# Two-layer LoRA residual kernel: the adapter ids are loaded by SP ahead of the first block of x, no longer by GpSimd

## The chip, the cores and the metric

One core of one Trainium2 chip runs the kernel. The metric is the device time of one execution in microseconds (us), taken as the median of several runs.

## The reference, cut to what matters

The input `x` has 8 batch rows of 512 tokens with 2048 features. Two residual steps follow each other. In the first, every batch row picks one of 8 small adapters (rank 16), by its entry in `itok_B_3_7`. In the second, there is a shared dense 2048 x 2048 product and a rank-16 adapter picked by `itok_B_0_15`.

```python
# step 0
Bx  = einsum('bni,bri->bnr', x, B0[ids0])
x   = x + einsum('bnr,bor->bno', Bx, A0[ids0])
# step 1
xr  = einsum('bsi,bir->bsr', x, lora_A[ids1])
x   = x + einsum('bsi,io->bso', x, W) + einsum('bsr,bro->bso', xr, lora_B[ids1])
```

So the program has to know the 16 integers `ids0` and `ids1` before it can fetch any adapter matrix. They are 8 int32 values each, 32 bytes.

## The kernel before, in words

**Tiling.** The 8 batch rows are worked in 4 pairs (`PAIRS`). For each pair, the dense product is a seven-product scheme in the manner of Strassen (`P1, P2, P6, P7, P4, P3, P5`, in this order), and each product has 8 units (`UNITS`). The identity is added to W's diagonal blocks, so that x + xW is one product. A unit is 24 matmuls of 128x128 by 128x512 in the loop of L1024. Every operand is split into a high and a low part in float32r: ScalarE casts the high part (`w_hi` L555, `b_hi` L566), VectorE subtracts to get the low part (`w_lo` L708, `b_lo` L721), and three matmuls stand for one.

**Folding step 0 in.** In the first pair, products P1, P2, P7 and P4 carry extra matmuls: `p_mm` (L997) multiplies the block of W that is in SBUF by the adapters A0 of all 8 batch rows side by side (`a0_hi`, `a0_lo`), and `in_mm` (L955) multiplies the chosen B0 and A1 by x into `lr_ps`. `p_mm` of unit 0 stands directly behind the 24 matmuls of unit 0 in TensorE's program. It waits for `a0_ready`, which VectorE gives after `a0_split` (L784), which follows ScalarE's `a0_split` (L582), which waits for all eight A0 loads together (`a0_loaded` at 16 * NB).

**Who loads what.** There is one order per engine, written out by hand.

- GpSimd (POOL) builds `eye` (L312, L314), loads the ids (L385, L386), waits for both, then reads each id into a register (`value_load`, L318 and L321) and issues one load for it: 8 loads of A0 (L389, 128 KB each, written into `a0_raw`, which is a view of `u3`; the profile calls it `u`), two loads of `in_raw` (L327), 8 loads of A1 (L393). Later come eight late A0 loads (L417), eight copies of B1 from HBM to HBM (L420), and the stores of the results.
- SP issues all loads of x (`load_x`, L442) and of W (`load_raw`, L480), each 512 KB. The program begins with x block 0, W block 0, x 1, W block 2, x 2, W block 1, x 3, W block 3. The W blocks go through a ring of four buffers `w_raw` (`RAWS`). In the first eight units each unit takes two of them: its own block, and a second one that VectorE turns into a difference (`w_second`, L714), that SP stores to HBM (`store_sum`, L487) for later use. The buffer of the second block is loaded again when that store has landed, and SP waits for it in order.

**VectorE around the change.** Before unit 0: the diagonal sum (L703), the low parts of x 0 and W 0 (L721, L708), then `w_second(0)` (L714), which needs W block 1. Then for unit 1: the diagonal sum, `w_lo`, `b_lo`, four small operations that build the base of `j_raw` (L894 to L901), and then `a0_split` twice and `in_split` (L799).

The two lines that move stand in GpSimd's program; the wait behind them stays:

```python
            pool.dma_start(ids[:, 0, :], ids0).then_inc(ids_loaded, 16)
            pool.dma_start(ids[:, 1, :], ids1).then_inc(ids_loaded, 16)
            pool.wait_ge(ids_loaded, 32)
```

Of the kernel before, what the change touches and what calls it, by code (L numbers as in the profile page):

```python
# [35 lines left out]
def lora_residual_program(nc, xT, ids0, ids1, A0n, B0, W, A1, B1, yT):  # L36
    NB = ids0.shape[1]
    NA0, _, C, R = A0n.shape
    NA1 = B1.shape[0]
    N = xT.shape[3]  # L40
# [112 lines left out]
    with ExitStack() as ctx:  # L153
        def sb(name, shape, dt=F32):
            return ctx.enter_context(nc.sbuf_tensor(name, shape, dt))
# [4 lines left out]
        def sem(name):  # L160
            return ctx.enter_context(nc.semaphore(name))
# [36 lines left out]
        ids = sb("ids", [1, 2, NB], I32)  # L198
# [11 lines left out]
        ids_loaded = sem("ids_loaded")  # L210
# [100 lines left out]
        def _(pool):  # L311
# [18 lines left out]
            def load_lr(i):  # L330
                p, b, half, _ = lr_plan[i]
                if i == 0:
                    pool.wait_ge(b1_copied, 16 * NB)
                    pool.wait_ge(a0_ready, 4 * len(P_PRODUCTS))
                else:
                    pool.wait_ge(lr_ready, i)
                for h in ((0, 1) if b else (half,)):
                    for g in range(2):
                        pool.wait_ge(*stage_free(stage_at["pst", h, g]))
                for c in range(4):  # L340
                    pool.dma_start(lr_raw[2 * R * c:2 * R * (c + 1), :], lrw[2 * p + b, :, half * HD:(half + 1) * HD]  # L341
                                   ).then_inc(lr_loaded, 16)
                if (b, half) == (1, 0):
                    for s in range(2):
                        last = max(k for k, (kind, q, _) in enumerate(stage_plan) if k % STAGES == s and q <= p
                                   or k % STAGES == s and kind == "pst")
                        pool.wait_ge(*stage_free(last))
                    for c in range(4):
                        pool.dma_start(lr_more[2 * R * c:2 * R * (c + 1), :], lrw[2 * p + b, :, HD:D]
                                       ).then_inc(lr_more_loaded, 16)  # L350
# [31 lines left out]
                pool.wait_ge(*bank_free(tile(p, P5, m)))  # L382
                pool.dma_start(yT[(2 * p + 1) * C + m, :, :], u2[:, m, :]).then_inc(u2_stored[m], 16)

            pool.dma_start(ids[:, 0, :], ids0).then_inc(ids_loaded, 16)  # L385
            pool.dma_start(ids[:, 1, :], ids1).then_inc(ids_loaded, 16)  # L386
            pool.wait_ge(ids_loaded, 32)
            for b in range(NB):
                pool.dma_start(a0_raw[:, b, :, :], A0n[bass.ds(id0(b), 1), :, :, :].rearrange("a p c r -> (a p) c r")  # L389
# [46 lines left out]
        def _(sp):  # L436
            def load_x(p, i, j):
                if p:
                    user = {X11: P5, X12: P7, X21: P4, X22: P3}[i]
                    sp.wait_ge(x_ready, 4 * ((p - 1) * PRODUCTS + user) + j + 1)  # L440
                half, b = divmod(i, 2)
                sp.dma_start(x_raw[i][:, 2 * j:2 * j + 2, :], xT[(2 * p + b) * HC + 4 * half + j, :, :, :]  # L442
                             ).then_inc(x_loaded[i][j], 16)
# [17 lines left out]
            def load_raw(r):  # L461
                n = raw_plan[r]
                p, o, u = at(n)
                if r >= RAWS:
                    raw_free(r - RAWS)
                block = {P1: A11, P2: A12, P6: A22, P4: A22, P3: A12, P5: A21}.get(o)
                kind = {P6: None if p == 0 else S2, P7: S3}.get(o)
                if raw_of[n] != r:
                    block = {P1: A21, P5: A22}.get(o)
                    kind = {P6: S3, P3: S2}.get(o)  # L470
                if kind is None:
                    src = W[block, u, :, :, :]
                else:
                    if kind == S3:
                        k = raw_of[u] + 1
                        sp.wait_ge(w_stored[k % RAWS], 16 * s3_stores[k])
                    else:
                        sp.wait_ge(s2_stored[u % 2], 16 * (u // 2 + 1))
                    src = w_sum[kind, u, :, :, :]
                sp.dma_start(w_raw[r % RAWS][:, :, :], src).then_inc(w_loaded[r % RAWS], 16)  # L480
# [8 lines left out]
            def load_fix(q):  # L489
# [4 lines left out]
                sp.wait_ge(*stage_free(stage_at["c21" if q >= UNITS else "c11", 0, q % UNITS]))  # L494
                sp.dma_start(stage[s % STAGES][:, :], c_kept[q, :, :]).then_inc(fix_loaded[s % STAGES], 16)

            load_x(0, X11, 0)
            load_raw(0)
            load_x(0, X11, 1)
# [183 lines left out]
        def _(dve):  # L683
# [167 lines left out]
            def fix(q):  # L851
                s = stage_at["fix", 1, q]
                dve.wait_ge(fix_loaded[s % STAGES], 16 * sum(k == "fix" for k, _, _ in stage_plan[s % STAGES:s + 1:STAGES]))
                dve.wait_ge(fix_mm_done, q + 1)
                dve.tensor_tensor(stage[s % STAGES][:, :], (j_ps, p_ps)[q % 2][:, :], stage[s % STAGES][:, :], ALU.add
                                  ).then_inc(fix_done, 1)
# [232 lines left out]
```

## Time and profile before

| | |
|---|---|
| median of 3 runs | 1403.8 us (1402.41 to 1404.17) |
| profiled execution, its own time | 1402.34 us |
| span of the profiled execution | 1400.7 us |
| TensorE busy | 1367.2 us, 98% of the span |
| VectorE, ScalarE, GpSimd busy | 58%, 29%, 12% |
| mean granted TensorE clock | 0.993 |
| mean DMA traffic | 187 GB/s |

TensorE is busy in all of the span but some 33 us by the first line (matmul records overlap and some can be missing, so the waits are read from the waits' own view). The span runs from the first to the last instruction; the profiled execution took 1.6 us more than its span. Engines are PE (TensorE matmul), PEld (its weight load), DVE (VectorE), ACT (ScalarE), POOL (GpSimd) and SP. A "q" behind a name is the engine's instruction queue, where DMA issues, register loads and waits are handled. "Landing" is the time from a DMA's issue to its semaphore.

### The profile page before, as it was taken

To read this page: it belongs to the slowest core of one execution; us is meant where nothing else is said; L and a number is where in the kernel's file an instruction comes from. 1 tells how busy PE (TensorE), PEld (TensorE's weight loads), DVE (VectorE), ACT (ScalarE), POOL (GpSimd) and SP (SyncE) were. 2 spreads that over 40 slices of the span, in tenths; PEclk is the share of its full clock that TensorE was granted. 3 is DMA by queue.
4 is the path that set the end of the run, shared out by engine and by line. 5 is a ranking of instruction groups with operands and counts; after the bars stand their busy time and mean duration, and the time that the engine had idled before them with its cause. 6 is when DMAs were issued, how large, how long until landed. Compare 5 with 4: busy or idle time off the path is not lost.

```text
span 1400.7 us, 15653 instructions
## 1 busy us (share of the span) xinstructions
PE 1367.2 (98%) x6016; PEld 1129.2 (81%) x6016; DVE 810.2 (58%) x941; ACT 405.9 (29%) x462; POOL 165.0 (12%) x317
## 2 busy tenths in 40 slices
PE   5999999999999999999999999999999999999997
PEld 4888888888878888888887888888887888888886
DVE  3455855357776455646775555555766445554675
ACT  2332222223234223322332323232322422232230
POOL 3200100111123010012011010012012001001202
PEclk8999999999999999999999999999999999999999
DMA  8864843458887343357684252446785334234755
GB/s 303 310 225 134 299 158 113 153 186 280 294 280 240 122 136 120 129 195 246 236 289 146 86 173 96 151 151 213 256 297 187 99 120 135 91 91 133 223 201 180
DMA packets 76778, 261.81 MB, mean 187 GB/s; under 512 B 12176, under 2 KB 12176, under 8 KB 76576
## 3 DMA queue, kind: packets, MB, share of 16 engines
q1 hardware_dynamic: 57600, 205.55, 43.5%
q0 software_dynamic: 19104, 55.27, 11.7%
q8 instruction: 48, 0.79, 0.2%
q14 instruction: 26, 0.21, 0.0%
HBM read 213.52 MB, written 48.30 MB: 187 GB/s over the span
## 4 chain that ended last, share of the span: by engine, by line
PE 85%; DVE 5%; DMA 5%; ACT 2%; issue 2%; POOL 0%; POOLq 0%; SPq 0%; ACTq 0%; DVEq 0%
PE y_ps L1024 76%; PE lr_ps L955 4%; PE p_ps L997 3%; DMA w_raw<-in_W 2%; PE y_ps L976 2%; ACT w_hi L555 2%; DVE w_lo L708 1%; DVE w_raw L694 1%; DVE b_lo L721 1%; DMA w_raw<-w_sum 1%; DVE u L776 1%; DMA stage_all<-lrw 0%; DMA u<-in_A0n 0%; DVE u L777 0%; DVE val L835 0%
## 5 line engine op out<-in xcount | busy, mean ns | idle before, releaser
L1024 PE MATMUL y_ps<-b_hi,w_hi 128*128 128x512 f32 x1792 | 699.3, 390 | 15.3 <-DVE w_lo L708 8.8
L1024 PE MATMUL y_ps<-b_lo,w_hi 128*128 128x512 f32 x1792 | 698.6, 390 | 0.0
L1024 PE MATMUL y_ps<-b_hi,w_lo 128*128 128x512 f32 x1792 | 698.4, 390 | 0.0
L708 DVE TENSOR_TENSOR w_lo<-w_raw,w_hi 128x1024 fp32r<-128x1024 f32 x216 | 264.6, 1225 | 460.9 <-ACT w_hi L555 460.9
L555 ACT CAST w_hi<-w_raw 128x1024 fp32r<-128x1024 f32 x216 | 227.6, 1054 | 879.5 <-PE y_ps L1024 474.9
L1024 PEld LDWEIGHTS y_ps<-b_hi,w_hi 128*128 128x128 f32 x1792 | 337.3, 188 | 86.6 <-DVE w_lo L708 8.8
L1024 PEld LDWEIGHTS y_ps<-b_hi,w_lo 128*128 128x128 f32 x1792 | 337.2, 188 | 70.2
L1024 PEld LDWEIGHTS y_ps<-b_lo,w_hi 128*128 128x128 f32 x1792 | 337.3, 188 | 70.1
L721 DVE TENSOR_TENSOR b_lo<-x_raw,b_hi 128x1024 fp32r<-128x1024 f32 x112 | 136.5, 1219 | 0.0
L566 ACT CAST b_hi<-x_raw 128x1024 fp32r<-128x1024 f32 x112 | 117.5, 1049 | 2.4 <-DMA x_raw<-in_xT 2.4
L694 DVE TENSOR_TENSOR w_raw<-w_raw 128x1024 f32<-128x1024 f32 x64 | 78.1, 1221 | 19.5 <-DMA w_raw<-in_W 11.6
L377 POOL DMA_DIRECT2D out_y<-stage_all x64 | 34.9, 546 | 413.9 <-DVE stage_all L760 377.9
L760 DVE TENSOR_TENSOR stage_all<-y_ps,u 128x512 f32<-128x512 f32 x64 | 43.1, 688 | 20.8 <-PE y_ps L976 16.9
L955 PE MATMUL lr_ps<-b_hi,in_stk 128*128 128x512 f32 x128 | 50.4, 394 | 0.0
L955 PE MATMUL lr_ps<-b_lo,in_stk 128*128 128x512 f32 x128 | 50.3, 393 | 0.0
L381 POOL DMA_DIRECT2D out_y<-u x32 | 17.6, 548 | 260.1 <-DVE u L776 259.5
L769 DVE TENSOR_TENSOR u<-y_ps,u 128x512 f32<-128x512 f32 x64 | 41.1, 685 | 7.4 <-PE y_ps L1024 5.0
L976 PE MATMUL y_ps<-val,lr_w 128*128 128x512 f32 x112 | 44.0, 393 | 1.3 <-DVE val L835 1.1
L327 POOL DMA_DIRECT2D in_raw<-in_B x8 | 4.5, 563 | 307.6 <-issue 307.6
L341 POOL DMA_DIRECT2D lr_raw<-lrw x64 | 31.4, 497 | 76.1 <-DVE lr_w L817 68.6
L997 PE MATMUL p_ps<-w_hi,a_hi 128*128 128x512 f32 x64 | 26.0, 407 | 8.2 <-DVE a_lo L784 8.2
L955 PEld LDWEIGHTS lr_ps<-b_hi,in_stk 128*128 128x128 f32 x128 | 24.5, 191 | 5.2
(81 smaller groups left out, 605.8 us busy)
## 6 DMA issues: line engine op xcount, KB each, us to landing
w_raw<-in_W SPq DMA_DIRECT2D x208, 512.0 KB, 3.8
w_raw<-w_sum SPq DMA_DIRECT2D x96, 512.0 KB, 3.6
x_raw<-in_xT SPq DMA_DIRECT2D x64, 512.0 KB, 5.4
out_y<-u POOLq DMA_DIRECT2D x64, 256.0 KB, 6.4
out_y<-stage_all POOLq DMA_DIRECT2D x64, 256.0 KB, 3.4
lr_raw<-lrw POOLq DMA_DIRECT2D x64, 128.0 KB, 4.0
w_sum<-w_raw SPq DMA_DIRECT2D x8, 512.0 KB, 6.2
c_kept<-stage_all POOLq DMA_DIRECT2D x16, 256.0 KB, 3.2
```

The source lines that it names most:

```text
L377: pool.dma_start(dst, stage[s % STAGES][:, :]).then_inc(stage_stored[s % STAGES], 16)
L555: act.copy(w_hi[n % 2][:, :, :], w_tile(n)[:, :, :]).then_inc(w_hi_done, 1)
L566: act.copy(b_hi[:, 2 * j:2 * j + 2, :], x_raw[i][:, 2 * j:2 * j + 2, :]).then_inc(x_hi_done, 1)
L694: last = dve.tensor_tensor(raw[:, :, :], w_raw[main_raw(n)][:, :, :], w_raw[r % RAWS][:, :, :], ALU.subtract if o == P3 else ALU.add)
L708: dve.tensor_tensor(w_lo[n % 2][:, :, :], w_tile(n)[:, :, :], w_hi[n % 2][:, :, :].bitcast(F32), ALU.subtract).then_inc(w_ready, 1)
L721: dve.tensor_tensor(b_lo[:, 2 * j:2 * j + 2, :], x_raw[i][:, 2 * j:2 * j + 2, :], b_hi[:, 2 * j:2 * j + 2, :].bitcast(F32), ALU.subtract). ...
L760: dve.tensor_tensor(stage[s % STAGES][:, :], bank[:, :], (u2 if o == P2 else u3)[:, m, :], ALU.add).then_inc(added, 1)
L769: dve.tensor_tensor(u2[:, m, :], bank[:, :], u2[:, m, :], ALU.add).then_inc(added, 1)
L955: last = pe.matmul(lr_ps[:, :], cols, x[:, c, :], start=(first and c == 0 and x is b_hi), stop=(half == 1 and c == HC - 1 and x is b_lo))
L976: return pe.matmul(out[:, :], lr_w[i % 2][:, m * P:(m + 1) * P], val[b][:, :], start=start, stop=True)
L997: last = pe.matmul(p_ps[:, :], a0[:, 2 * j + c, :], w[n % 2][:, c, :], start=(j == 0 and c == 0 and k == 0), stop=(j == 3 and c == 1 and k ...
L1024: last = pe.matmul(bank[:, :], w[n % 2][:, c, t * P:(t + 1) * P], x[:, 2 * j + c, :], start=(j == 0 and c == 0 and w is w_hi and x is b_hi ...
```

## The change

The two loads of the ids leave GpSimd's program. SP issues them, ahead of everything else. GpSimd's wait for `ids_loaded` stays where it was, and nothing else is different. Line numbers behind the removed lines are lower by two in GpSimd's part and in the part of SP ahead of the inserted lines.

```diff
@@ GpSimd
-            pool.dma_start(ids[:, 0, :], ids0).then_inc(ids_loaded, 16)
-            pool.dma_start(ids[:, 1, :], ids1).then_inc(ids_loaded, 16)
             pool.wait_ge(ids_loaded, 32)
             for b in range(NB):
...
@@ SP
+            sp.dma_start(ids[:, 0, :], ids0).then_inc(ids_loaded, 16)
+            sp.dma_start(ids[:, 1, :], ids1).then_inc(ids_loaded, 16)
             load_x(0, X11, 0)
             load_raw(0)
             load_x(0, X11, 1)
```

GpSimd's order at its start, before. `TENSOR_LOAD ids` is the read of one id into a register, and `u` is the A0 buffer:

```order
L314 AFFINE_SELECT eye<-eye 128x128
L385 DMA ids<-in_ids 1x8x1
L386 DMA ids<-in_ids 1x8x1
L318 TENSOR_LOAD ids
L318 ISA x2
L389 ISA
L389 DMA u<-in_A0n 128x256
```

and with the change:

```order
L314 AFFINE_SELECT eye<-eye 128x128
L318 TENSOR_LOAD ids
L318 ISA x2
L387 ISA
L387 DMA u<-in_A0n 128x256
L318 TENSOR_LOAD ids
```

The two DMA issues between `eye` and the first read of an id are gone from GpSimd.

SP's order at its start, before:

```order
L435 UNCONDITIONAL_BRANCH
L442 DMA x_raw<-in_xT 128x1024
L480 DMA w_raw<-in_W 128x1024
L442 DMA x_raw<-in_xT 128x1024
L480 DMA w_raw<-in_W 128x1024
L442 DMA x_raw<-in_xT 128x1024
```

and with the change:

```order
L433 UNCONDITIONAL_BRANCH
L495 DMA ids<-in_ids 1x8
L496 DMA ids<-in_ids 1x8
L440 DMA x_raw<-in_xT 128x1024
L478 DMA w_raw<-in_W 128x1024
L440 DMA x_raw<-in_xT 128x1024
```

Every x and W load of SP stands behind two more issues. The orders of TensorE, VectorE and ScalarE are the same in both kernels.

## Rows read from the trace of the kernel before

**Rows 1.** The page: busy time, share of the span, instructions of TensorE
```profile
PE 1367.2 (98%) x6016; PEld 1129.2 (81%) x6016; DVE 810.2 (58%) x941; ACT 405.9 (29%) x462; POOL 165.0 (12%) x317
```

**Rows 2.** The three largest waits of TensorE: total us, times, longest us
```profile
PE y_ps L1024 <- DVE w_lo L708: 8.8, 1, 8.8
PE p_ps L997 <- DVE a_lo L784: 8.2, 1, 8.2
PE y_ps L1024 <- DVE u L777: 6.4, 3, 2.2
```

**Rows 3.** Chain of waits, first 84 us: start us, us, what
```profile
2.31 5.29 DMA ids<-in_ids
...
17.54 6.19 DMA u<-in_A0n
...
24.19 0.44 DVE a_lo L784
...
24.67 2.92 PE p_ps L997 x6
...
35.18 1.36 PE p_ps L997 x6
```

**Rows 4.** Timeline of GpSimd: start us, us, what, [idle before <-releaser]
```profile
2.31 0.55 POOL L386 DMA_DIRECT2D ids<-in_ids  x1
9.10 0.59 POOL L389 DMA_DIRECT2D u<-in_A0n  x1 [6.25 <-issue]
...
30.29 0.54 POOL L393 DMA_DIRECT2D u<-in_A  x1 [1.57 <-issue]
```

**Rows 5.** Timeline of SP's queue
```profile
0.94 0.38 SPq L442 DMA_DIRECT2D x_raw<-in_xT  x1
...
1.85 0.42 SPq L442 DMA_DIRECT2D x_raw<-in_xT  x1
...
12.72 3.90 SPq L480 DMA_DIRECT2D w_raw<-in_W  x2
...
27.09 0.33 SPq L487 DMA_DIRECT2D w_sum<-w_raw  x1
```

**Rows 6.** Timeline of ScalarE
```profile
4.61 1.04 ACT L566 CAST b_hi<-x_raw 128x1024 fp32r<-128x1024 f32 x1 [2.40 <-DMA x_raw<-in_xT]
...
38.78 1.05 ACT L589 CAST lr_w<-u 128x1024 fp32r<-128x1024 f32 x1
...
60.39 1.05 ACT L555 CAST w_hi<-w_raw 128x1024 fp32r<-128x1024 f32 x1 [6.87 <-PE p_ps L997]
```

**Rows 7.** Landing times of the eight A0 loads (L389)
```profile
DMA to landing us min/median/max: 3.3/4.6/6.2
```

**Rows 8.** Timeline of VectorE
```profile
11.09 1.23 DVE L714 TENSOR_TENSOR w_raw<-w_raw 128x1024 f32<-128x1024 f32 x1 [2.30 <-DMA w_raw<-in_W]
...
14.98 1.22 DVE L721 TENSOR_TENSOR b_lo<-x_raw,b_hi 128x1024 fp32r<-128x1024 f32 x1
...
16.70 0.24 DVE L901 COPY j_raw<-j_raw 128x64 f32<-128x64 f32 x1
...
57.57 0.49 DVE L703 TENSOR_TENSOR w_raw<-w_raw,eye 128x128 f32<-128x128 f32 x2 [1.65 <-DMA w_raw<-in_W]
```

**Rows 9.** Timeline of TensorE: the last matmul of unit 0
```profile
16.09 0.39 PE L1024 MATMUL y_ps<-b_hi,w_lo 128*128 128x512 f32 x1
```

**Rows 10.** Stretches: us; PE, PEld, DVE, ACT, POOL busy; granted clock, DMA share, GB/s
```profile
9.00:12.00 3.00, 3.00 (x8) 2.35 (x9) 0.91 (x1) 0.00 (x0) 1.68 (x3) 1.00 1.02 416
...
24.70:29.70 5.00, 5.00 (x12) 3.93 (x13) 3.13 (x5) 2.50 (x5) 2.15 (x4) 0.50 0.65 182
30.00:34.00 4.00, 4.00 (x19) 3.29 (x18) 2.54 (x3) 0.00 (x0) 1.87 (x4) 1.00 1.01 363
...
402.10:405.30 3.20, 3.20 (x8) 2.52 (x9) 1.69 (x3) 0.28 (x1) 2.31 (x5) 0.50 0.93 278
430.00:1380.00 950.00, 944.74 (x4163) 780.64 (x4162) 556.14 (x633) 283.36 (x313) 97.26 (x186) 1.00 0.51 170
```

## The prediction, made before the changed kernel ran

> **What bounds the kernel now.** I read the page first. TensorE is busy for 98% of the span [rows 1], so time is only to be had where TensorE waits, or where its clock is halved. The second view was the list of its waits [rows 2]: 8.8 us before the first matmul, 8.2 us at the first `p_mm`, 6.4 us in three pieces at the ends of pairs. What follows in the list is smaller than any of these. After 24.67 us TensorE runs through the rest of the program with little more than 6.4 us of waits, so an early gain should reach the end unless a buffer or a load is late in its turn.
>
> The third view was the chain of waits in the first 84 us [rows 3]. The wait of 8.2 us ends last on this chain: GpSimd issues the second ids load at 2.31; it takes 5.29 us to land, until 7.60; GpSimd reads an id and issues a load of A0 for it, eight times, the first at 9.10 [rows 4] and the eighth at 17.54; the eighth takes 6.19 us to land; ScalarE and VectorE split it; `p_mm` starts at 24.67. TensorE's last matmul of unit 0 was issued at 16.09 and done at 16.48 [rows 9]. So the ids stand at the head of the only long wait in the program's middle, and this is where the change acts.
>
> **The change, step by step.** *Removed from GpSimd:* two issues, the second of 0.55 us [rows 4]. They lie wholly inside its wait for the ids and cost nothing by themselves; what counts is when the second lands.
>
> *Added to SP:* two issues ahead of x. SP starts at 0.94, and the x loads at 0.94 and 1.85 have one W issue between them, so two issues take 0.91 us [rows 5]. The second ids load is thus issued near 1.40, and everything of SP moves by 0.91 us. The first matmul waits for x 0 and W 0 with nothing to cover it: 8.8 [rows 2] becomes 9.7, and unit 0 ends at 17.4 in place of 16.48 [rows 9]. This cost is hidden as long as `p_mm` starts later than 17.4; if A0 were there by then, 0.91 us would be the price.
>
> *When the ids land.* The trace has no small load on SP's queue. Nearest is the first x load, also at the head of that queue: issued at 0.94, its reader ScalarE starts at 4.61 [rows 5, 6], so 3.67 us, of which its 524 kB take 1.3 us at 416 GB/s [rows 10]. That leaves 2.4 us for one of 32 bytes. From the other side: the 5.29 us that the same bytes take now. I take 2.4, because the x row shares queue, place and an idle start, while the ids of before go beside 512 KB loads. So the ids land near 3.8 (bounds 3.8 and 6.7), 3.8 us before 7.60.
>
> *The A0 loads.* GpSimd's own pace does not change, so the eighth is issued at 17.54 - 3.8 = 13.7. Its landing takes 3.3 to 6.2 us, median 4.6 [rows 7]; `p_mm` starts 0.94 us behind it (17.54 + 6.19 = 23.73, and 24.67 [rows 3]). That gives 17.9 to 20.8, with the median 19.2.
>
> *VectorE's own order, which is late next.* Its `a0_split` stands behind its work for unit 1. That begins with `w_second(0)` at 11.09, which waited for W block 1, and ends with the last `j_raw` copy at 16.94 [rows 8], 5.85 us later. W block 1 is the sixth load of SP. It moves by 0.91 us, and by the A0 bytes that now go in front of it: some 6 loads of 131 kB at 416 GB/s, 1.9 us (bounds: none, and all eight, 2.5 us). Hence 11.09 + 0.91 + 1.9 = 13.9, VectorE free for A0 at 19.75, and `p_mm` 0.48 us later (a_lo at 24.19 to 24.67 [rows 3]): 20.2, between 18.3 and 20.8. Both chains end near each other, and the later one counts. **I take 20.4.** TensorE resumes 24.67 - 20.4 = **4.3 us earlier**, and its gap shrinks from 8.2 to 3.0 us. The cover of what was moved past is then thin, but there: b_lo of unit 1 was done at 16.2 [rows 8] and comes at 19.0, while unit 1's matmuls start after `p_mm` and `in_mm`, past 22.
>
> *The clock.* After the 8.2 us gap TensorE works at half clock (1.2 of 2.4 GHz): granted 0.50 from 24.70 to 29.70 and 1.00 from 30.00 on [rows 10], and six `p_mm` matmuls take 2.92 us where they take 1.36 later [rows 3]. The half-clock stretch reaches from 24.67 to some point between 29.7 and 30, 5.2 us, of which half, 2.6 us, is lost. What a 3.0 us gap does is not shown. Below it there are the three gaps of 2.0 to 2.2 us at pair ends [rows 2]: the first was followed by 3.2 us or a little more at 0.50, the other two lie in a stretch with a granted clock of 1.00 throughout [rows 10]. So the loss is between 0 and 2.6 us. I take the stretch of the nearest gap that had one, 3.4 us, 1.7 us lost. That is a gain of **0.9 us** (bounds 0 and 2.6). If the clock stays up, `in_mm` waits some 0.3 us for `in_split`, which stands behind `a0_split`.
>
> *The rest.* GpSimd's A1, late A0 and B1 loads come 3.8 us earlier by the clock, TensorE's need of them 5.2 us earlier. A1 is needed first: its last load was issued at 30.29 [rows 4] and ScalarE read it at 38.78 [rows 6]. Now the issue is at 26.5, and the read comes 5.2 us earlier, at 33.6: 7.1 us between them, more than any of the A0 landings. So this costs nothing. The W ring is a rival below.
>
> *Sum.* 4.3 + 0.9 = 5.2 us. The profiled execution would take 1402.34 - 5.2 = 1397.1. It was 1.5 us quicker than the median of the runs, so the median becomes 1403.8 - 5.2 = **1398.6 us**. A measurement of this kernel can tell about 0.2%, 2.8 us, from no change; 1401.0 and 1406.6 are the borders.
>
> **Rivals.**
>
> *The clock stays up* (chance 0.23). The 3.0 us gap is no fall, as with two of the three gaps at pair ends. Gain 4.3 + 2.6 - 0.3 = 6.6 us: 1397.2. Against it speaks that a gap of 2.0 us was enough once [rows 2, 10].
>
> *The ids are hardly earlier* (chance 0.15): a load of one row takes its 5.3 us on whatever queue, because the time lies in the round trip and not in the traffic beside it. Then they land at 1.40 + 5.3 = 6.7, 0.9 us earlier; `p_mm` starts near 23.7, and the gap of 6.3 us still halves the clock: 1402.9, no change. For it: no row shows how much of the 5.29 us was traffic. Against it: the x load's 3.67 us in total. The Trainium skill ("DMA: Bandwidth & Descriptors", Specifications) puts the two queues' first bytes only some 0.4 us apart, about 1 us and 0.6 us. By that page alone, an estimate, the ids would come 0.9 + 0.4 = 1.3 us earlier and the kernel would take about 1402.5. No row has a small load on both queues, so the trace neither agrees nor disagrees.
>
> *The W ring decides* (chance 0.06), the one on the other side. In the first eight units each buffer of a second block waits for a store to land before it is loaded again. VectorE already waited 1.65 us for W block 12 at 57.57; its sum was done at 58.06, and the cast that needs it was released by TensorE at 60.39 [rows 6, 8]: 2.3 us of cover. In this rival the ring is paced by DMA, not by TensorE. It starts 0.9 us later, has 1.9 us of A0 traffic in front of its first reload (at 12.72 before [rows 5]), and the B1 copies now overlap it more. As soon as block 12 is over 2.3 us later than before by the clock, all that was gained at 20 us is waited for there; 1.2 us more and a new half-clock stretch of 3.4 us (1.7 us lost) give 1403.8 + 1.2 + 1.7 = 1406.7. Against it: SP issued its last reload by 16.6 and the x load behind it, and then nothing until 27.09 [rows 5], waiting for VectorE, which waited for A0. That part of the ring moves forward with the change.
>
> **How the numbers follow.** Forecast (short gap, one short half-clock stretch): 0.56. Clock up: 0.23. Ids hardly earlier: 0.15, of which 0.05 for landings in between that still give over 2.8 us. Ring: 0.06, of which 0.02 for a loss that only eats the gain. Faster: 0.56 + 0.23 + 0.05 = 0.84; within: 0.10 + 0.02 = 0.12; slower: 0.04. The range: at best both chains end early (19.2, a gain of 5.5) and the clock stays up (2.6 - 0.3): 7.8 us, 1396.0. At worst within 8 in 10, the ids land halfway between the bounds (5.2, so 1.5 us later than I take) and the clock gives nothing: 4.3 - 1.5 = 2.8 us, 1401.0; I add 0.5 us, since the three runs lie 1.8 us apart. Range 1395.9 to 1401.5.
>
> **What would show it.** In the profile of the changed kernel: ids issued at about 0.94 and 1.40, landing after 2.4 us each; the first A0 load at 5.3 and the eighth at 13.7; the first matmul at 9.7; `w_second(0)` at 13.9; `p_mm` at 20.4, released by VectorE, behind a gap of 3.0 us; a half-clock stretch of about 3.4 us or none; no other wait of TensorE before the first pair's end. It would be wrong if the ids landed after 5.2, if `w_second(0)` began after 16, or if waits of TensorE for w_lo appeared between 28 and 75 us.

## The result, and the profile after

| | before | changed |
|---|---|---|
| median of 20 runs each | 1402.68 us | 1398.18 us |
| lowest and highest | 1399.11 to 1407.09 | 1392.75 to 1404.54 |
| profiled execution, own time | 1402.34 us | 1396.92 us |
| its span | 1400.7 us | 1395.3 us |

The ratio of changed to before is 0.9969, with a 95% interval of 0.9956 to 0.9981: a gain of 4.3 us, between 2.7 and 6.2. The changed kernel is faster, by less than the spread of single runs.

The waits of TensorE in the changed kernel (total us, times, longest), to be read against [rows 2]:

```profile
PE y_ps L1024 <- DVE w_lo L708: 9.6, 1, 9.6
PE y_ps L1024 <- DVE u L777: 6.8, 3, 2.5
PE p_ps L997 <- DVE a_lo L784: 2.3, 1, 2.3
PE y_ps L976 <- DVE val L835: 0.8, 2, 0.6
```

The wait at `p_mm` went from 8.2 to 2.3 us, the one before the first matmul grew from 8.8 to 9.6. The others are nearly as they were.

The timeline of SP's queue and of GpSimd (start us, us, what), against [rows 4, 5]:

```profile
0.94 0.34 SPq L495 DMA_DIRECT2D ids<-in_ids  x1
1.33 0.22 SPq L496 DMA_DIRECT2D ids<-in_ids  x1
1.60 0.36 SPq L440 DMA_DIRECT2D x_raw<-in_xT  x1
...
4.05 0.71 POOL L387 DMA_DIRECT2D u<-in_A0n  x1 [2.56 <-issue]
...
12.09 0.54 POOL L387 DMA_DIRECT2D u<-in_A0n  x1 [0.61 <-issue]
```

The ids' landing has no row of its own here, but GpSimd's reads of the ids show when they were there. The group of these reads on the tile `ids`, with its minimum, median and maximum in ns and its first and last start:

```profile
L318 POOLq TENSOR_LOAD <-ids x9: 288/294/501, 2.5 to 12.1; - x9
```

The first read is at 2.5 us, 1.2 us after the second ids load was issued. Before, it was at 7.6. All A0 loads follow over 5 us earlier: the first at 4.05 in place of 9.10, the eighth at 12.09 in place of 17.54.

The timeline of VectorE, against [rows 8]:

```profile
13.24 1.23 DVE L714 TENSOR_TENSOR w_raw<-w_raw 128x1024 f32<-128x1024 f32 x1 [3.73 <-DMA w_raw<-in_W]
...
18.85 0.20 DVE L901 COPY j_raw<-j_raw 128x64 f32<-128x64 f32 x1
18.96 0.75 DVE L784 TENSOR_TENSOR a_lo<-u,a_hi 128x256 fp32r<-128x256 f32 x2
...
56.62 0.49 DVE L703 TENSOR_TENSOR w_raw<-w_raw,eye 128x128 f32<-128x128 f32 x2 [3.02 <-DMA w_raw<-in_W]
...
66.42 0.49 DVE L703 TENSOR_TENSOR w_raw<-w_raw,eye 128x128 f32<-128x128 f32 x2 [3.62 <-DMA w_raw<-in_W]
```

VectorE goes from the `j_raw` copy straight into `a0_split`, with no idle time between them. So its own order sets `p_mm` now, not the landing of A0. That order begins with the landing of W block 1, which the chain of waits shows:

```profile
3.91 9.31 DMA w_raw<-in_W
13.22 0.02 issue
13.24 1.23 DVE w_raw L714
```

The last two rows of the timeline are the W ring at units 6 and 7: VectorE waits 3.0 and 3.6 us there for W blocks, where unit 6 had 1.65 us in [rows 8].

The stretches of TensorE's granted clock around `p_mm`, in the columns of [rows 10]:

```profile
19.50:20.20 0.70, 0.70 (x3) 0.60 (x4) 0.21 (x1) 0.24 (x1) 0.24 (x1) 1.00 1.02 392
20.40:23.60 3.20, 3.20 (x8) 2.11 (x8) 2.74 (x4) 2.20 (x4) 1.38 (x4) 0.50 0.95 346
23.80:30.00 6.20, 6.20 (x29) 5.11 (x28) 2.79 (x4) 0.18 (x1) 2.32 (x6) 1.00 0.86 308
```

After a gap of 2.3 us the first three matmuls run at the full clock, then the clock is halved for some 3.4 us.

**Where the gain is, along the program.** The chain of waits gives the start of each piece of TensorE's work. In the changed kernel:

```profile
19.43 2.21 PE p_ps L997 x6
21.64 1.96 PE lr_ps L955 x4
23.60 5.59 PE y_ps L1024 x24
...
31.46 5.44 PE y_ps L1024 x24
...
69.42 5.69 PE y_ps L1024 x24
...
79.00 5.44 PE y_ps L1024 x24
```

and before:

```profile
29.30 5.87 PE y_ps L1024 x24
...
37.44 5.44 PE y_ps L1024 x24
...
75.39 5.46 PE y_ps L1024 x24
...
84.75 5.44 PE y_ps L1024 x24
```

The lead of the changed kernel, by how much earlier it starts the same piece, is 5.24 us at `p_mm` (24.67 against 19.43), 5.70 at unit 1, 5.98 at unit 2 once the clock is back in both, 5.97 at unit 7, 5.75 at the first unit of P2, and 5.4 at the end. Unit 7 takes 5.69 us where it took 5.46: the first 0.2 us are lost there, in a short wait for `w_lo` that the list of waits above does not have:

```profile
69.36 0.19 PEld L1024 LDWEIGHTS y_ps<-b_hi,w_hi 128*128 128x128 f32 x1 [0.38 <-DVE w_lo L708]
```

### The profile page after: what moved, and what is told of

Same layout as the page of the kernel before. It is cut to its first block, busy times and chain, and to the rows that moved or that the text cites. A ratio compares the mean times of both kernels' runs of the same rounds, so it can differ in the third digit from the quotient of the medians.

```text
span 1395.3 us, 15653 instructions
## 1 busy us (share of the span) xinstructions
PE 1366.9 (98%) x6016; PEld 1128.3 (81%) x6016; DVE 810.1 (58%) x941; ACT 404.9 (29%) x462; POOL 163.3 (12%) x315
## 4 chain that ended last, share of the span: by engine, by line
PE 84%; DVE 7%; DMA 4%; ACT 2%; issue 2%; SPq 0%; POOLq 0%; POOL 0%; ACTq 0%; DVEq 0%
PE y_ps L1024 74%; PE lr_ps L955 4%; PE p_ps L997 3%; DMA w_raw<-in_W 3%; ACT w_hi L555 2%; DVE w_lo L708 2%; DVE w_raw L694 2%; PE y_ps L976 2%; DVE b_lo L721 1%; DVE u L776 1%; DVE u L777 1%; DMA w_raw<-w_sum 1%; DVE w_raw L703 0%; DVE val L835 0%; PE j_ps L1005 0%
## 5 line engine op out<-in xcount | busy, mean ns | idle before, releaser
L694 DVE TENSOR_TENSOR w_raw<-w_raw 128x1024 f32<-128x1024 f32 x64 | 78.2, 1221 | 19.7 <-DMA w_raw<-in_W 12.2
L703 DVE TENSOR_TENSOR w_raw<-w_raw,eye 128x128 f32<-128x128 f32 x96 | 23.5, 287 | 14.0 <-DMA w_raw<-in_W 13.3
```

What stands on the lines that cost most here:

```text
L694: last = dve.tensor_tensor(raw[:, :, :], w_raw[main_raw(n)][:, :, :], w_raw[r % RAWS][:, :, :], ALU.subtract if o == P3 else ALU.add)
```

## The experiments

**Is it the queue or the traffic?** *The ids on GpSimd, as its first work.*

```diff
+            pool.dma_start(ids[:, 0, :], ids0).then_inc(ids_loaded, 16)
+            pool.dma_start(ids[:, 1, :], ids1).then_inc(ids_loaded, 16)
             pool.memset(eye[:, :], 1.0).then_inc(eye_done, 1)
...
-            pool.dma_start(ids[:, 0, :], ids0).then_inc(ids_loaded, 16)
-            pool.dma_start(ids[:, 1, :], ids1).then_inc(ids_loaded, 16)
```

> GpSimd issues the ids loads as its first work, ahead of building eye (which it did before them), so about 0.7 us earlier than in the kernel before and ahead of the first bytes of x; x stays where it was. Theory traffic (the ids were slow because x and W were moving beside them): the first issue comes near 0.93, the second near 1.6; the second still lands with traffic beside it from about 3.3 us on, so GpSimd reads the first id between 4.5 and 6 us, not at 7.6. Rival queue (a small load of GpSimd takes 5 us whatever moves): read at 1.6 + 5.3 = 6.9 us. In either case the first matmul stays at 8.8 us.

Measured: GpSimd issued them at 1.5 and 2.15 us, hardly earlier than before (1.62 and 2.31). The chain shows 5.13 us of landing for the second, the first read came at 7.31, and `p_mm` at 23.78. One run took 1403.85 us. The numbers look like the rival's, but the traffic beside the load was the same as before, so this run does not tell the two apart. It does show that the place in GpSimd's order is worth 0.3 us.

*SP issues nothing before the ids of GpSimd have landed.*

```diff
+            sp.wait_ge(ids_loaded, 32)
             load_x(0, X11, 0)
             load_raw(0)
```

> The kernel before, with one wait added: SP issues nothing until the ids of GpSimd have landed. This measures a GpSimd load of 32 bytes with nothing beside it, and costs the first matmul what it takes. Theory traffic: the second ids load (issued at 2.31) lands after 2 to 2.5 us, near 4.5 us; SP's first issue is then at 4.5, the first matmul at 12.5, the first A0 load at 6. Rival queue: it lands at 7.6 as before, SP's first issue is at 7.6, the first matmul at 15.5.

The chain of waits of this kernel:

```profile
2.31 1.60 DMA ids<-in_ids
```

against 2.31 and 5.29 in [rows 3]. The same engine, queue, bytes and time of issue, and 1.6 us in place of 5.3 with nothing beside it. **Some 3.7 us of the ids' landing was traffic.** SP's first issue came at 3.93, the first matmul at 11.79, the first A0 load at 5.42, `p_mm` at 22.0. The rival falls. The one execution took 1399.92 us, with the first matmul 3.0 us later than before and `p_mm` 2.7 us earlier.

*The ids on SP, behind x block 0 and W block 0.*

```diff
-            sp.dma_start(ids[:, 0, :], ids0).then_inc(ids_loaded, 16)
-            sp.dma_start(ids[:, 1, :], ids1).then_inc(ids_loaded, 16)
             load_x(0, X11, 0)
             load_raw(0)
+            sp.dma_start(ids[:, 0, :], ids0).then_inc(ids_loaded, 16)
+            sp.dma_start(ids[:, 1, :], ids1).then_inc(ids_loaded, 16)
```

> The changed kernel, with the two ids loads of SP behind x block 0 and W block 0 in place of ahead of them. Theory traffic: the ids are issued near 1.9 and 2.2 with 1 MB in front of them and land behind it, near 6 us; first matmul at 8.85; first A0 load at 7.6, eighth at 15.7, p_mm near 21.5. Rival queue (SP's queue is quick for small loads wherever they stand): they land 1.2 us after issue, near 3.5; first A0 load at 5, p_mm at 18.8, and this order would beat the change by 0.7 us.

```profile
2.22 3.90 DMA ids<-in_ids
```

The same queue as in the changed kernel, 0.9 us later in it, and 3.90 us in place of 1.2. The first A0 load was at 7.68, the eighth at 15.72, `p_mm` at 22.10, the first matmul at 8.80, and the one execution took 1399.38 us. So the place ahead of x is what makes SP's load quick.

**What does SP's delay cost?** *The kernel before, with SP loading the ids a second time into a buffer that nobody reads.*

```diff
+            sp.dma_start(ids_x[:, 0, :], ids0).then_inc(ids_x_loaded, 16)
+            sp.dma_start(ids_x[:, 1, :], ids1).then_inc(ids_x_loaded, 16)
             load_x(0, X11, 0)
...
```

> The kernel before, where SP loads the ids into a spare buffer that nobody reads, ahead of x. This is the cost of the change without its benefit. Theory (the delay of SP is hidden behind the wait for A0): first matmul at 9.5 us (8.8 plus two issues), ids read by GpSimd at 7.6 or up to 0.7 later, p_mm at 24.7, time as before. Rival (the two issues are paid in full): p_mm and the end come 0.7 us later.

The first matmul came at 9.47. But `p_mm` did not stay at 24.7: it came at 22.32. The chain shows where the 2.35 us are:

```profile
2.31 4.36 DMA ids<-in_ids
...
17.22 4.16 DMA u<-in_A0n
```

GpSimd's own ids loads landed 0.9 us sooner, of which 0.3 are left at the issue of the eighth A0 load (17.22 against 17.54). The other 2.0 us are the landing of that load, 4.16 us in place of 6.19. That x, issued 0.66 us later, left them less traffic is a likely reason, but one execution does not show it. The delay of SP is hidden, as the theory had it. The one run took 1404.63 us, inside the range of the kernel before.

This also bounds what the ids are worth. The three profiles with the ids on GpSimd's queue beside SP's x have `p_mm` at 24.67, 23.78 and 22.32. The two with SP's ids first and the same work behind them (the changed kernel, and below the one with x12 and x22 later) have it at 19.43 and 19.54. The profile before is the latest of the first three, because its eighth A0 load took the longest to land. So of the 5.24 us at `p_mm` up to 2.35 may belong to that execution and not to the place of the ids.

**Is VectorE late because of the A0 bytes?** *GpSimd holds A0 back until `w_second(0)` is done.*

```diff
             pool.wait_ge(ids_loaded, 32)
+            pool.wait_ge(postsum_done, 1)
```

> The changed kernel, where GpSimd issues no A0 load before VectorE has finished w_second(0), so that no A0 byte moves ahead of W block 1. Theory (in the changed kernel the A0 bytes in front delay W block 1 by some 1.5 us): w_second(0) starts at 11.09 + 0.66 = 11.75 us, not at 13.24. TensorE then waits for A0 instead: first A0 load near 14.5, p_mm near 29, and the time is some 9 us worse than the changed kernel. Rival (it is later for another reason, such as slower DMA in this run): w_second(0) stays near 13.2.

```profile
12.00 1.23 DVE L715 TENSOR_TENSOR w_raw<-w_raw 128x1024 f32<-128x1024 f32 x1 [2.46 <-DMA w_raw<-in_W]
```

`w_second(0)` starts at 12.00 in place of 13.24 (the line number is one higher here): A0 in front of W block 1 costs 1.2 us. That is 0.25 us later than expected. `p_mm` came at 26.57, earlier than the 29 expected, since the eighth A0 load landed within 2.3 us of its issue at 23.37 in place of over 5. The execution took 1406.11 us.

**Does VectorE's order set `p_mm`?** *The `j_raw` operations one unit later.*

```diff
-                    if n == 0:
+                    if n == 1:
                         half = j_raw[:, :, :, :]
```

> The changed kernel, with the four small VectorE operations on j_raw (0.8 us) moved from unit 0's turn to unit 1's, so that a0_split does not stand behind them. Theory (in the changed kernel VectorE's own order sets p_mm, not A0): p_mm starts at 18.6 in place of 19.4 us, released by a_lo; about 0.8 us gained there, which no timing resolves (within 0.2% of the changed kernel). Rival (the A0 landing at 17.4 is the limit): p_mm stays at 19.4.

The waits of TensorE that differ, and the clock from 17 to 30 us:

```profile
PE p_ps L997 <- DVE a_lo L784: 1.1, 1, 1.1
PE lr_ps L955 <- DVE in_stk L799: 1.1, 1, 1.1
```

```profile
17.00:30.00 13.00, 10.86 (x47) 8.34 (x46) 8.31 (x15) 4.17 (x8) 5.36 (x10) 1.00 0.94 349
```

`p_mm` starts at 18.77, 0.66 us earlier, so VectorE's order was the limit. TensorE then waits at `in_mm`, because `in_raw` is the next load to be late. In these 13 us the clock did not fall (later it did, at the first pair's end: 0.50 from 397.1 to 400.3), and the span was 1392.4 us. Timed, it took 1397.67 us (10 runs), 0.9965 of before (0.9952 to 0.9978): not to be told from the changed kernel.

**Another idle engine.** *The ids on ScalarE's queue.*

```diff
-            sp.dma_start(ids[:, 0, :], ids0).then_inc(ids_loaded, 16)
-            sp.dma_start(ids[:, 1, :], ids1).then_inc(ids_loaded, 16)
...
+            act.dma_start(ids[:, 0, :], ids0).then_inc(ids_loaded, 16)
+            act.dma_start(ids[:, 1, :], ids1).then_inc(ids_loaded, 16)
             w_split_first = -1
```

> The ids are loaded by ScalarE, which is idle at the start; SP's and GpSimd's programs have no ids load. Theory (what counts is that nothing moves beside them yet, not that SP does it): GpSimd reads the first id near 2.5 us as in the changed kernel, and SP's x is not delayed: first matmul at 8.85 and not 9.56, w_second(0) at 12.6 and not 13.2, p_mm at 18.8 and not 19.4. The time is 0.6 us better than the changed kernel, 4 to 5 us better than before. Rival (x's issue beside it makes the ids slow again): read of the id after 4 us, p_mm after 20.

The rival held for the read: issued at 0.9 and 1.5 us, with SP's x issued at the same time, the ids were read at 4.4 us and not at 2.5. The first matmul was at 8.77, `w_second(0)` at 11.35, and `p_mm` at 19.89, now behind the A0 landing. The ratio was 0.9986 (0.9970 to 1.0002), median 1401.22 in 12 runs: a gain is not shown, and the runs reached from 1394.2 to 1404.7.

> The kernel with the ids on ScalarE's queue once more, for a second profile, since its runs ranged from 1394 to 1405. If the ids' landing is a matter of chance there (their issue lies beside x's first bytes), the read of the first id moves by over 0.5 us against 4.4 us; if it stays, the spread has another source, such as the clock.

In the second profile the read came at 4.8 us, and `p_mm` at 19.96, within 0.1 us of the first. Yet the span was 1401.1 us and not 1393.2. The stretches behind `p_mm`, of the first profile:

```profile
19.90:22.90 3.00, 2.92 (x6) 1.81 (x6) 0.73 (x3) 0.75 (x3) 1.18 (x4) 0.50 0.95 373
23.30:30.00 6.70, 6.70 (x30) 5.55 (x31) 4.78 (x5) 1.86 (x3) 2.78 (x6) 1.00 0.77 255
```

and of the second:

```profile
20.00:28.80 8.80, 7.30 (x16) 5.25 (x17) 5.47 (x8) 2.91 (x5) 3.64 (x7) 0.50 0.81 261
29.40:35.00 5.60, 5.60 (x26) 4.59 (x25) 0.00 (x0) 0.34 (x1) 2.14 (x4) 1.00 0.96 290
```

The same program, nearly the same gap (3.4 and 3.9 us), and behind `p_mm` the clock was half for about 3 us in one execution and 9 us in the other. Unit 2 starts at 32.15 and at 35.53, so 3.4 us of the 7.9 are there already; 1.1 of them are a longer wait at `in_mm` (1.5 us against 0.4), the rest is mostly the clock. The other 4.5 come at later pair ends: their waits for L777 sum to 4.9 and 6.5 us, the second profile has one more wait of 1.2 us for `w_lo` there, and one more half-clock stretch (401.3 to 404.5), which costs 1.7.

**The W ring.** *`p_mm` of unit 0 left out.*

```diff
-                    p_mm(n, a, g, j).then_inc(unit_done, 1)
+                    if n > 0:
+                        p_mm(n, a, g, j).then_inc(unit_done, 1)
...
```

> The changed kernel without p_mm in unit 0 (six matmuls, 1.4 us, left out; the sum for step 0 lacks its first two chunks). TensorE then has no wait for A0 and goes on to in_mm, which waits for in_split at about 21.4, and after that to unit 1. Theory of the W ring (its cover in the changed kernel is 2 to 2.5 us at unit 6 and gone at unit 7): TensorE gets about 1.4 to 2 us ahead and then waits for w_lo at units 6 and 7, so by unit 8 the lead over the changed kernel is under 1 us. Rival (the ring moves forward with TensorE): no wait, and the lead of 1.4 us or more stays.

```profile
PE lr_ps L955 <- DVE in_stk L799: 3.2, 1, 3.2
PE y_ps L1024 <- DVE w_lo L708: 1.9, 1, 1.9
```

The second wait is at unit 7 (71.50 us), behind VectorE's diagonal sum at 68.56, which had waited 3.85 us for W block 14. Unit 7 starts 2.1 us later than in the changed kernel, although work was left out. The expected lead was gone before the ring mattered: the clock was at 0.50 from 22.3 to 25.5, and unit 2 starts at 31.52 against 31.46. W block 14 itself came 2.1 us later than in the changed kernel (68.56 against 66.42), and no run shows why. The holding back of x above also has a wait at unit 7, of 2.0 us.

*The same, with SP's loads of x12 and x22 moved from units 4 to 7 to units 6 to 9.*

```diff
-                    if o == P1 and u >= 4:
-                        load_x(0, X12, u - 4)
-                        load_x(0, X22, u - 4)
+                    if 6 <= n < 10:
+                        load_x(0, X12, n - 6)
+                        load_x(0, X22, n - 6)
```

> The kernel without p_mm in unit 0, and SP's eight loads of x12 and x22 moved from units 4 to 7 to units 6 to 9, so that less moves beside the W ring when blocks 12 and 14 are due. (Left out: p_mm of unit 0, as before.) Theory of the W ring (the wait of 1.9 us for w_lo at unit 7 is the ring's reloads and stores slowed by those x loads): the wait at unit 7 goes, VectorE's diagonal sum for unit 7 comes 2 us or more earlier than 68.6, and no wait of the same size comes at units 8 to 12. Rival (the wait comes from elsewhere, or x then comes late for the t3 sums): still over 1 us of waits between 55 and 100 us.

VectorE's timeline, once without and once with the move:

```profile
68.56 0.49 DVE L703 TENSOR_TENSOR w_raw<-w_raw,eye 128x128 f32<-128x128 f32 x2 [3.85 <-DMA w_raw<-in_W]
```

```profile
62.28 0.49 DVE L703 TENSOR_TENSOR w_raw<-w_raw,eye 128x128 f32<-128x128 f32 x2
```

The block is there 6 us earlier, and TensorE has no wait between `in_mm` and 100 us. So it was the ring, slowed by x loads that nobody needed yet. The clock stayed halved longer after this run's gap of 3.9 us (unit 1 took 7.45 us), and still the first unit of P2 starts at 80.14, 1.0 us ahead of the run without the move (81.12). The execution as a whole took 1400.53 us against 1399.21. So 2.3 us were lost further on: the waits for L835 sum to 2.8 us against 0.6, and those for L777 to 5.9 against 5.6.

*The changed kernel with the move alone.*

> The changed kernel with the same move of the x12 and x22 loads and nothing else. Theory (in the changed kernel the ring has no cover left at unit 7, and some executions lose there): the diagonal sum of unit 7 comes before 65.5 in place of 66.4 us; the profile is within 0.3 us of the changed one otherwise, and the median is 0 to 1.5 us better than 1398.2. Rival (the ring costs the changed kernel nothing): same median within 0.5 us.

VectorE's diagonal sum for unit 7 comes at 62.27 in place of 66.42, and unit 7 takes 5.46 us again. The median was 1397.62 us in 12 runs, ratio 0.9968 (0.9956 to 0.9981). The cover is back, and the 0.6 us against 1398.18 are inside the spread.

*Both moves.*

> The changed kernel with both the j_raw operations one unit later and the x12 and x22 loads later. Theory: the 0.7 us gained at p_mm and the smaller chance of a half-clock stretch (gap 1.1 us) add to what the ring gives: median near 1396 to 1397, 6 to 7 us better than before. Rival (neither is on the path): as the changed kernel, 1398.

Median 1397.31 us in 7 runs, ratio 0.9966 (0.9948 to 0.9985). It beats the kernel before; over the changed one no gain is shown. Its profile had the clock halved for some 3 us behind a `p_mm` gap of 2.2 us, where the `j_raw` move alone had none behind 1.1 and 1.1 us. Yet `p_mm` starts at the same time in both, 18.81 and 18.77. The gap differs because unit 0 ends earlier here: its last matmul was issued at 16.23 and not at 17.32. TensorE from 9.7 to 15.0 us, in the `j_raw` run and then here:

```profile
9.70:15.00 5.30, 5.30 (x13) 4.20 (x14) 1.63 (x3) 0.06 (x1) 2.37 (x5) 1.00 1.03 393
```

```profile
9.70:15.00 5.30, 5.30 (x18) 4.24 (x19) 1.63 (x3) 0.03 (x1) 2.37 (x5) 1.00 1.03 391
```

There are 13 matmuls against 18. Unit 0's matmuls take 0.63 us each at first and 0.39 later, and the step comes at 14.5 us in one execution and at 12.2 in the other (at 13.2 in the changed kernel's), although the granted clock in both rows is 1.00. So the `j_raw` move takes 0.7 us off the gap. The rest of what made it 1.1 us came from when unit 0's matmuls became quick in that execution, and with it perhaps the clock that stayed up.

## Why the prediction was right, point by point

- **The end result.** Forecast 1398.6 us, 1395.9 to 1401.5, faster with a chance of 0.84. Measured 1398.18. The forecast gain was 5.2 us, the measured one 4.3 (2.7 to 6.2), and 5.4 between the two profiled executions. That the time is within 0.4 us is partly luck: the forecast started from a median of 3 runs, 1403.8, which is 1.1 us above the median of 20, and it took off 0.7 to 0.9 us too much.
- **The bound.** The wait at `p_mm` hung on the ids, and moving them moved it: 24.67 to 19.43 us, with one reserve: the profile before has the latest `p_mm` of the three with the ids on GpSimd's queue. Against the earliest of them (22.32) the move is worth 2.9 us there, not 5.2.
- **The landing of the ids, mis-sized.** The step took the x load's 3.67 us less its bytes, 2.4 us, as the lower bound too. Issue to read was 1.2 us, below that bound. The x row was the wrong relative: besides its bytes it held time that a load of 32 bytes does not have. A bound from "nothing at all" would have been needed below. The error did not reach the sum, since VectorE's order and not A0 set `p_mm`.
- **The price of two issues.** 0.66 us (x at 1.60 in place of 0.94), not 0.91, and 0.72 us at the first matmul (9.56 against 8.84). Small loads issue quicker (0.22 us for the second) than the 512 KB ones that gave the term.
- **The A0 loads.** The eighth was issued at 12.09, not 13.7. ScalarE's cast for it began at 17.48, so some 5.4 us of landing, where 4.6 had been taken; the profile lists 5.3 to 6.1 us for these loads. These two errors work against each other.
- **VectorE next.** The forecast said both chains end near each other and VectorE's is the later one, at 20.2. It was at 19.43, released by VectorE. The term for A0 bytes was 1.9 us; the hold-back run gives 1.2. This and the price of the issues are what made the forecast of 20.4 a microsecond late.
- **The clock.** One short half-clock stretch was the likeliest case, 1.7 us lost; one of 3.4 us came, though it began only at 20.3 and not with `p_mm`. Its gain is the lead at unit 2 less the lead at `p_mm`, 5.98 - 5.24 = 0.7 us, against 0.9. The case "clock stays up" (0.23) was met in the `j_raw` run and with x held back, not in the changed kernel's profile.
- **The lower end of the range** takes ids that land 1.5 us late off the gain in full. By the forecast's own terms A0 would then be ready for a `p_mm` at 19.2 + 1.5 = 20.7, only 0.3 us behind the 20.4 that was taken. The range was wider there than its reasons.
- **The rival "ids hardly earlier"** fell: without traffic even GpSimd's load took 1.6 us. With no bulk transfer ahead of it, the second ids load landed after 1.60 us on GpSimd's queue (x held back) and after 1.15 us on SP's (`1.33 1.15 DMA ids<-in_ids` in the chain of the `j_raw` run); in the second case x was issued at 1.60, before it landed. The Trainium skill ("DMA: Bandwidth & Descriptors", Specifications) gives the two queues' first bytes as about 1 us and 0.6 us, and the difference of 0.45 us here agrees with that. The mistake of that rival was to take the queue, or the round trip, for what had made the 5.3 us.
- **The W ring** was nearer than a chance of 0.06 says, though its price of several us did not come. One of the forecast's signs of being wrong, a wait for `w_lo` between 28 and 75 us, did appear, 0.38 us long at 69.36. The ring's cover at unit 6 was reckoned as 2.3 us, but the critical block is the one of unit 7: in the changed profile its `w_lo` ended at 69.31 and unit 7 started at 69.36. The forecast looked at block 12 because the profile before shows a DMA wait there and none at block 14. What a further microsecond at `p_mm` would lose there is open. The run with `p_mm` left out waited 1.9 us at unit 7. But the `j_raw` run, with the x loads in their old place, reached unit 7 at 68.38, 1.0 us ahead of the changed kernel, and lost nothing there (5.46 us), since its diagonal sum came at 64.81 and not at 66.42.

What stays open: where the 0.9 us between the gain of the two profiles (5.4) and the gain of the medians (4.5) lies. Single executions of either kernel differ by over 7 us, and the half-clock stretches with the pair ends, shown in the two profiles of one program, are large enough for it, and so is the late A0 landing in the profile before. That this is all of it was only argued.

## What to carry to other kernels

A tiny load at the head of a long dependent chain belongs ahead of the first bulk transfer: most of what it waits for is the traffic beside it. Being first on another queue is not the same, as ScalarE's shows: with x issued at the same time on SP's, the landing took 2.9 and 3.3 us in place of 1.2. When such a chain becomes shorter, ask at once which engine's own order is next (here VectorE's `j_raw` work ahead of `a0_split`), and which ring of buffers had been filled during the wait that is gone. That ring's cover is to be read at each of its blocks, not only at the one that waits now.

## What the runs showed of the hardware that was not expected

- 32 bytes took 5.3 us from issue to landing on GpSimd's queue beside 512 KB loads of SP, and 1.6 us when SP had issued nothing yet. On SP's queue it was 3.9 us behind 1 MB and 1.2 us ahead of it. On ScalarE's queue, with SP's first x issue at the same time, issue to read took 2.9 us.
- The same program gave half-clock stretches of some 3 and 10 us (0.50 from 19.9 to 23.2, and from 19.0 to 29.0, in the two profiles with ScalarE's queue), with gaps of 3.4 and 3.9 us. Gaps of 1.1 us (the `j_raw` run) and of 1.9 us (x held back) at `p_mm` left the clock at 1.00; gaps of 2.2, 2.3 and 2.5 us (both moves, the changed kernel, x12 and x22 later) were each followed by about 3.4 us at 0.50. At the pair ends the length of the gap did not decide: in the profile before, the clock fell behind 2.0 us and stayed up behind 2.2 and 2.2; in the changed kernel's it fell behind 2.4 us (0.50 from 730.4 to 733.6) and stayed up behind 1.8 and 2.5 (1.00 from 1060 to 1070).
- In the changed kernel the clock fell while TensorE was already working again, under 1 us after `p_mm` had begun (19.43; still 1.00 until 20.2, and 0.50 from 20.4 on).
